# Storing 21 groups of the turned adjacency as fp32 words in place of fp16 pairs

## What is computed

```python
# one: hyperbolic mean
XW = mobius_matvec(W, X); gamma = 2.0 / (1.0 - sum(XW * XW))
two_mean = (A_hat @ (gamma * XW)) / (A_hat @ (gamma - 1.0))
# two: symmetric normalisation
support = norm_adj @ x;  out = support @ W.T + b
# three: diffusion and attention masked by adj
diffusion = adj_norm @ x - x
attn = softmax(beta * (x @ x.T / norms) * adj, axis=1)
out = diffusion + sigmoid(alpha) * (attn @ x - x)
# four: messages into a GRU cell
agg = adj @ states;  msg = relu(agg @ W_msg.T + b_msg);  out = gru(msg, states)
```

## Time and profile before

| | us |
|---|---|
| median of 3 runs | 1311.12 (1306.46 to 1311.75) |
| the profiled execution | 1309.65 |
| its span, first to last instruction | 1307.9 |
| PE busy | 1227.0 (94%) |
| DVE busy | 770.7 (59%) |
| ACT busy | 685.3 (52%) |
| POOL busy | 460.1 (35%) |

### The profile page before, as it was taken

The page is one execution under the profiler, slowest core; times in us unless marked ns, Lnnn a source line. Parts: engine busy times, 40 slices in busy tenths (PEclk is TensorE's granted clock), DMA queues, the critical chain, the costliest instruction groups (busy, mean ns, idle before and its releaser), DMA issues.

```text
span 1307.9 us, 20934 instructions
## 1 busy us (share of the span) xinstructions
PE 1227.0 (94%) x7980; PEld 789.5 (60%) x7980; DVE 770.7 (59%) x1769; ACT 685.3 (52%) x995; POOL 460.1 (35%) x433
## 2 busy tenths in 40 slices
PE   5889999999999989869999999999999889999996
PEld 4888888887884544425555656555655544444442
DVE  6856665655643352687787878787878860122213
ACT  6555555555442222168778787878787530123222
POOL 4012231222123232325566665657565560000000
PEclk9899999999999999979999999999999999999998
DMA  9999999999978979466777777877776849978870
GB/s 304 358 416 415 406 397 377 386 350 357 352 288 320 387 299 353 177 241 247 269 265 274 258 268 267 285 268 287 269 278 213 302 178 365 390 272 315 312 267 24
DMA packets 113524, 394.20 MB, mean 301 GB/s; under 512 B 9872, under 2 KB 23440, under 8 KB 91536
## 3 DMA queue, kind: packets, MB, share of 16 engines
q1 hardware_dynamic: 105232, 388.80, 79.7%
q10 hardware_dynamic: 8192, 4.06, 1.1%
HBM read 319.95 MB, written 72.88 MB: 300 GB/s over the span
## 4 chain that ended last, share of the span: by engine, by line
PE 78%; DVE 8%; ACT 5%; DMA 4%; issue 4%; POOL 2%; POOLq 0%; SPq 0%; ACTq 0%; DVEq 0%
PE strip_b L688 8%; PE acc L629 6%; PE acc L630 6%; PE acc L636 6%; PE acc L707 4%; PE acc L705 4%; PE acc L704 4%; PE acc L703 4%; PE acc L605 4%; PE mid L605 4%; PE strip_b L580 3%; PE strip_a L580 3%; PE acc L603 2%; PE mid L603 2%; PE strip_a L671 2%
## 5 line engine op out<-in xcount | busy, mean ns | idle before, releaser
L1224 POOL TENSOR_TENSOR parts<-arena,parts 128x512 f16<-128x512 f32 x237 | 275.6, 1172 | 196.3 <-ACT parts L980 192.4
L980 ACT ACTIVATE parts<-arena 128x512 f16<-128x512 f32 x256 | 158.5, 624 | 111.1 <-DVE arena L1635 102.6
L1635 DVE SCALAR_TENSOR_TENSOR arena<-parts,dis,strip_b 128x512 f32<-128x512 f16 x256 | 188.9, 743 | 29.7 <-PE strip_b L688 22.5
L629 PE MATMUL acc<-arena,Y 128*128 128x512 f16 x428 | 162.8, 380 | 3.5 <-DMA arena<-adj_t 2.0
L688 PEld LDWEIGHTS strip_b<-ident,arena 128*128 128x128 f32 x1024 | 128.2, 142 | 60.9 <-DVE arena L1626 5.4
L688 PE MATMUL strip_b<-ident,arena 128*128 128x128 f32 x1024 | 155.4, 275 | 8.8 <-ACT arena L975 5.7
L630 PE MATMUL acc<-arena,Y 128*128 128x512 f16 x428 | 162.6, 380 | 0.0
L636 PE MATMUL acc<-arena,Y 128*128 128x512 f16 x428 | 162.5, 380 | 0.0
L969 ACT ACTIVATE arena<-arena,neg_peak 128x2048 f32<-128x2048 f32 x64 | 127.3, 1989 | 5.2 <-DVE neg_peak L1605 5.2
L1201 POOL TENSOR_TENSOR sc<-sc,power 128x4 f32<-128x4 f32 x31 | 31.5, 1016 | 279.6 <-DVE sc L1454 279.6
L975 ACT ACTIVATE arena<-arena,weight 128x2048 f32<-128x2048 f32 x57 | 113.4, 1989 | 2.6 <-DVE weight L1619 2.6
(11 more groups left out here) (332 smaller groups left out, 2559.1 us busy)
## 6 DMA issues: line engine op xcount, KB each, us to landing
arena<-adj_t SPq DMA_DIRECT2D x107, 1024.0 KB, 6.0
arena<-in_adj SPq DMA_DIRECT2D x64, 1024.0 KB, 9.5
arena<-in_adj SPq DMA_DIRECT2D x128, 512.0 KB, 5.8
parts<-adj_t SPq DMA_DIRECT2D x128, 512.0 KB, 7.3
adj_t<-parts SPq DMA_DIRECT2D x37, 1024.0 KB, 8.2
adj_t<-arena SPq DMA_DIRECT2D x27, 1024.0 KB, 9.2
scratch<-v ACTq DMA_DIRECT2D x8, 256.0 KB, 10.6
arena<-scratch SPq DMA_DIRECT2D x8, 256.0 KB, 4.6
```

The source lines that it names most:

```text
L629: pe.matmul(to, y_high, high, start=j == 2 * FIRST[l][s], stop=False)
L980: act.activation(part_h[:, b % 4, :], mixed[b % G_SLOTS], ACT.Copy).then_inc(high_done, 1)
L1224: pool.tensor_tensor(part_l[:, b % 4, :], mixed[b % G_SLOTS], part_h[:, b % 4, :], ALU.subtract).then_inc(low_done, 1)
L1635: dve.scalar_tensor_tensor(mixed[b % G_SLOTS], kept_slot(n % KEPT_SLOTS)[:, b % 2, 0, :], dis[:, j:j + 1], strip_b[:, b % 2, :], ALU.mult, ...
```

## The change

The 21 groups that layer two does not read back (`whole(s, g)`: g <= s - 2) are kept in DRAM as fp32 words, as many bytes as the two fp16 parts.

- Layer one: for these 42 pairs ACT first copies the scaled strip as fp32 into a ring slot of its own (`whole0`), then makes the high part from that slot into a second, "working" slot; DVE makes the low part from the two slots. PE's turn of pair n+2 waits for that copy and not for the low part. The whole slot is stored, the working slot is not; ring places are given in the order of the list `HOLDS`.
- Layer three: for the 84 whole blocks `mix` reads the fp32 block, and the product with the kept low part (L703) is left out.
- Layer four: for the 42 whole pairs ACT (`split3_high`) and DVE (`split3_low`) make high and low part in one of the six `kept_slot` places, one turn ahead in their programs; PE waits for that, and SP's next load into the slot waits for the split.

```diff
+def whole(s, g):
+    return g <= s - 2
+HOLDS = []
+for _s in range(SLABS):
+    for _g in range(GROUPS):
+        HOLDS += [("working" if whole(_s, _g) else "pair", _s * GROUPS + _g)] \
+            + ([("whole", _s * GROUPS + _g)] if whole(_s, _g) else [])
+WHOLE3 = [n for n in range(TURNS3) if whole(TURNS[3][n][0], TURNS[3][n][1] // 2)]
...
+                elif l == 3 and 2 * (n - TURNED_SLOTS) in WHOLE3:
+                    sp.wait_ge(low3_done, WHOLE3.index(2 * (n - TURNED_SLOTS)) + 2)
...
-                    sp.wait_ge(low_done, 2 * n + 2)
-                    sp.dma_start(adj_t[s, c], ring_slot(n)).then_inc(stored[n % RING_SLOTS], 16)
+                    if whole(s, c):
+                        sp.wait_ge(whole_done, wholes_done(2 * n + 1))
+                        sp.dma_start(adj_t[s, c], ring_slot(n, "whole")).then_inc(stored[store_hold(n) % RING_SLOTS], 16)
+                    else:
+                        sp.wait_ge(low_done, 2 * n + 2)
+                        sp.dma_start(adj_t[s, c], ring_slot(n)).then_inc(stored[store_hold(n) % RING_SLOTS], 16)
...
-                if n >= 2:
+                if n >= 2 and is_whole((n - 2) // PAIRS, (n - 2) % PAIRS):
+                    pe.wait_ge(whole_done, wholes_done(n - 2))
+                elif n >= 2:
                     pe.wait_ge(low_done, n - 1)
...
+                if l == 3 and n in WHOLE3:
+                    pe.wait_ge(low3_done, WHOLE3.index(n) + 1)
+                    pair = kept_slot(WHOLE3.index(n) % KEPT_SLOTS)
...
-                pe.matmul(to, Y[:, j, YD:YD + D], kept_slot(b // 2 % KEPT_SLOTS)[:, b % 2, 1, :], start=j == 0, stop=False)
-                pe.matmul(to, Y[:, j, 0:D], part_h[:, b % 4, :], start=False, stop=False)
+                apart = not is_whole(s, j // 2)
+                if apart:
+                    pe.matmul(to, Y[:, j, YD:YD + D], kept_slot(b // 2 % KEPT_SLOTS)[:, b % 2, 1, :], start=j == 0, stop=False)
+                pe.matmul(to, Y[:, j, 0:D], part_h[:, b % 4, :], start=j == 0 and not apart, stop=False)
...
+            def whole0(n):
+                g = n // 2
+                act.wait_ge(turned_up, n + 1)
+                hold_free(hold_of(g, "whole"))
+                act.activation(whole_pair(ring_slot(g, "whole"), n), strip[n % 2][:], ACT.Copy,
+                               scale=A_SCALE).then_inc(whole_done, 1)
+
+            def split3_high(n):
+                at = WHOLE3.index(n)
+                act.wait_ge(group_in[n // 2 % TURNED_SLOTS], groups_loaded(3, n // 2))
+                act.wait_ge(product, product_base[3] + (WHOLE3[at - KEPT_SLOTS] + 1 if at >= KEPT_SLOTS else 0))
+                act.activation(kept_slot(at % KEPT_SLOTS)[:, :, 0, :],
+                               whole_pair(turned_in[:, n // 2 % TURNED_SLOTS, :], n), ACT.Copy).then_inc(high3_done, 1)
...
+                if is_whole(n // PAIRS, n % PAIRS):
+                    act.wait_ge(whole_done, wholes_done(n))
+                    act.activation(ring_pair(n)[:, :, 0, :], whole_pair(ring_slot(g, "whole"), n),
+                                   ACT.Copy).then_inc(high_done, 1)
...
+                if is_whole(s, m):
+                    whole0(n)
                 high0(n)
...
+                if n + 1 in WHOLE3:
+                    split3_high(n + 1)
                 for k, s in hooks(3, n - ACT_LEAD):
...
+                if is_whole(n // PAIRS, n % PAIRS):
+                    dve.tensor_tensor(pair[:, :, 1, :], whole_pair(ring_slot(n // 2, "whole"), n), pair[:, :, 0, :],
+                                      ALU.subtract).then_inc(low_done, 1)
...
+            def split3_low(n):
+                at = WHOLE3.index(n)
+                held = kept_slot(at % KEPT_SLOTS)
+                dve.wait_ge(high3_done, at + 1)
+                dve.tensor_tensor(held[:, :, 1, :], whole_pair(turned_in[:, n // 2 % TURNED_SLOTS, :], n), held[:, :, 0, :],
+                                  ALU.subtract).then_inc(low3_done, 1)
...
+                kept = kept_whole(n % KEPT_SLOTS)[:, b % 2, :] if is_whole(b // NB, j // 2) \
+                    else kept_slot(n % KEPT_SLOTS)[:, b % 2, 0, :]
-                dve.scalar_tensor_tensor(mixed[b % G_SLOTS], kept_slot(n % KEPT_SLOTS)[:, b % 2, 0, :], dis[:, j:j + 1],
+                dve.scalar_tensor_tensor(mixed[b % G_SLOTS], kept, dis[:, j:j + 1],
                                          strip_b[:, b % 2, :], ALU.mult, ALU.add).then_inc(mixed_done, 1)
...
+                if n + 1 in WHOLE3:
+                    split3_low(n + 1)
                 for k, s in hooks(3, n - DVE_LEAD):
```

More of the change, by code:

```diff
@@ L189, in spare, with hold_of, ring_slot, whole_pair @@
             return arena[:, FULL + SLAB * n:FULL + SLAB * (n + 1)]
-        def ring_slot(g):
-            at = g % RING_SLOTS
+        def hold_of(g, kind):
+            return [at for at, (what, one) in enumerate(HOLDS) if one == g and (what == "whole") == (kind == "whole")][0]
+        def ring_slot(g, kind="pair"):
+            at = hold_of(g, kind) % RING_SLOTS
             return ring_head[:, at, :] if at < 4 else ring_tail[:, at - 4, :]
+        def whole_pair(held, n):
+            return held[:, 2 * UNIT * (n % 2):2 * UNIT * (n % 2 + 1)].bitcast(F32).rearrange("p (b w) -> p b w", w=SLAB)
         def split_pair(held, n):
@@ L336, in split_done, with stores_until, last_stores, store_hold @@
             return PAIRS * SLABS + b + 1
-        def held_stored(g):
-            return stored[g % RING_SLOTS], 16 * (g // RING_SLOTS + 1)
+        def stores_until(hold):
+            return 16 * sum(HOLDS[at][0] != "working" for at in range(hold % RING_SLOTS, hold + 1, RING_SLOTS))
+        def last_stores(slot):
+            return 16 * sum(HOLDS[at][0] != "working" for at in range(slot, len(HOLDS), RING_SLOTS))
+        def store_hold(g):
+            return hold_of(g, "whole" if whole(g // GROUPS, g % GROUPS) else "pair")
+        def held_stored(g):
+            hold = store_hold(g)
+            return stored[hold % RING_SLOTS], stores_until(hold)
+        def wholes_done(n):
+            return sum(whole(i // PAIRS, i % PAIRS // 2) for i in range(n + 1))
+        def is_whole(s, m):
+            return whole(s, m // 2)
         def unit_of(k):
@@ L883, in y_high, with hold_free @@
                                scale=scale).then_inc(y_hi, 1)
+            def hold_free(hold):
+                if hold >= RING_SLOTS:
+                    what, one = HOLDS[hold - RING_SLOTS]
+                    if what != "working":
+                        act.wait_ge(stored[hold % RING_SLOTS], stores_until(hold - RING_SLOTS))
+                    if what == "whole":
+                        act.wait_ge(low_done, 2 * one + 2)
+                    else:
+                        act.wait_ge(product, 2 * one + 2)
+            def whole0(n):
[10 more added lines that the diff above has]
+                               whole_pair(turned_in[:, n // 2 % TURNED_SLOTS, :], n), ACT.Copy).then_inc(high3_done, 1)
             def high0(n):
```

22 lines of the change are left out of this document (14 added, 8 removed).

## The result

The changed kernel takes 1315.21 us (median of 12 runs) against 1309.13 us before: ratio 1.0045, 95% interval 1.0036 to 1.0055. The forecast was 1306 us; the true change is small, but it has the other sign. The profiled execution took 1316.75 us, span 1314.9, 7.0 us more than the span before. One execution of the experiments (of E12's ten) took 7343 us; the intervals leave it out, and without it E12's median is 1312.7.

A forecast was written before the change was run, and what follows sets the result against it. The prediction took PE to bound the kernel. Its terms, -10.9 - 1.5 + 6.3 + 1.5 = -4.6 us on the profiled 1309.65, gave 1305.0; with the runs' median 1.5 higher it forecast 1306 us, range 1297 to 1316.

The forecast's parts named there:

- second rival: Layer three: steps stay at 1.91 us because ACT and DVE cannot follow; +5.1 us, 1316 us, chance 0.15.
- the step that failed: Layer one, six slab entries: a second ACT copy makes PE stand 1.05 us longer each, +6.3 us (bounds +4, +11).
- signs of being wrong: PE waits on ACT or DVE inside layer one's or at most layer four's whole units, or layer-three steps near 1.95 us.
- Layer three, slabs 2 to 6: 60 whole blocks each drop a 0.216 us product, less 2.0 us lost in layer norm: -10.9 us (bounds -12.9, -2).
- Slab 7: Layer three's last slab: 24 dropped products, 5.2 us for PE, mostly limited by others: -1.5 us (bounds 0, -5.0).
- Both resources named: Layer three, slab 7: DVE (31.1 us busy) and DMA (31 us) leave at most 5.0 of 36.1 us.
- Layer four: The splits of 42 pairs are hidden except at turn 32, the first whole turn: +1.5 us (bounds 0, +3).
- The port: Layer one's slab changes: DVE's low part meets a POOL instruction, 0.78 us longer, 4.7 us in all; 1311 us, chance 0.07.
- ACT late in layer one: Doubled copies reach PE in every whole pair, up to 1.05 us each, 38 us more; 1344 us, chance 0.08.
- Layer three does not follow: Layer three: steps of 1.91 us, as ACT and DVE are at 90%; +5.1 us, 1316 us, chance 0.15.

The follow-up runs named there:

- E12: Kernel before, with half of an additional ScalarE copy (512 of 1,024 elements a partition) at each of six layer-one slab entries: 1312.9 us.
- E3: Kernel before, with ScalarE making the high part of pair 1 of slabs 2 to 7 in layer one twice: 1317.6 us.
- E7: Changed kernel, with layer three's left-out product replaced by one of the same size with other operands: 1324.0 us.
- E4: Changed kernel, with group 0 of each slab left as fp16 parts, so 15 fp32 groups in place of 21: 1306.2 us.
- E10: Changed kernel, with layer four's first six group loads issued behind layer three's last pair, not between its pairs: 1316.6 us.
- E1: Changed kernel, with the last slab's accumulators read one pair earlier in layer one: 1310.9 us.
- E11: Changed kernel, with layer four's splits put behind the row steps of the same turn, not ahead of them: 1315.2 us.
- E8: Changed kernel, without layer four's splits and the waits for them, fp32 words multiplied as they are: 1311.5 us.
- E5: Changed kernel, with whole groups from group 1 on and none in slab 7, so 10 groups in place of 21: 1304.6 us.
- E2: Kernel before, with the last slab's accumulators read one pair earlier in layer one, no fp32 group: 1306.8 us.
- E6: Changed kernel, with whole groups from group 1 on (15) and accumulators read one pair earlier in slabs 3 to 7: 1303.9 us.

## Why the prediction was wrong, point by point

Between the -4.6 us of the sum and the +7.0 of the profiles stand 11.6 us: 7.2 in layer one, 1.5 in layer three's slabs 2 to 6, 1.9 in slab 7 and 0.9 in layer four. The 1306 started from a median of three runs, 1311.12; twelve gave 1309.13, so the forecast looks about 2 us nearer than it was. That 1315.2 lies within 1297 to 1316 is luck: the top of that range came from the second rival, whose steps of 1.91 us did not occur.

**Layer one: the step that failed** is "6 x 1.05 = +6.3 us ... it does not come back", with +11 as its upper bound. Measured: +13.5. What was worked out of the earlier trace rows held: the place, the six entries, the order of the instructions and the length of the wait (2.45 against "about 2.3") were right, and 6 x 1.18 = 7.1 us are that term. The other 6.5 us are the clock: four falls of 1.6. The term took PE's idle time at a price of its own length and put what comes behind it at nothing; E3 and E12 show that behind waits of 2.32 us time is lost as well, at two entries of five, and behind waits of up to 1.93 us it isn't. Neither bound held such a thing, since the earlier trace rows showed clock 1.00 throughout layer one. With these 6.5 us the forecast of 1306 becomes 1312.5. None of the prediction's signs of being wrong appeared, since all of them were waits and steps, and none was the granted clock.

**Layer three, slabs 2 to 6: right, a little too high.** -9.4 against -10.9. Steps of 1.73 us and the price of a matmul are exact (E7). The layer norm took 60 x 0.216 - 9.4 = 3.5 us, not 2.0: 0.25 of them in slab 4, where none were expected, 1.1 in slab 5, as worked out, and 2.15 in slab 6. E4 loses the same 3.5 with 40 blocks.

**Slab 7: nothing, as one bound had it.** +0.4 against -1.5. Both resources named are behind it: with the loads out of the way 2.2 of the 5.2 us reach the end of the slab (E10), and the rest goes in PE's waits on GpSimd and VectorE.

**Layer four: right, as far as the splits go.** +2.0 and +0.4 later against +1.5. The splits' part is 1.1 us at turn 32 (1.3 to 1.6 in E1, E7 and E11), where the term had put it, and 0.3 at turn 85; both go in E8. The 0.85 ahead of turn 32 comes before any split and is 0.26 at most in E1, E7 and E11; what makes it stays open. At turn 32 the load landed at 1119.25, and PE was due at 1120.88 by its wait of 0.96: a lead of 1.6 us (1 was worked out) against a split of 2.3. What was costed at nothing, the row work queued behind the split, is what PE's record names there, 0.2 us after the split's own data.

**The rivals.** The port: no low part at an entry was lengthened (VectorE's instruction of slab 6 takes 1.23 us). The rule cited (the Trainium skill, SBUF — State Buffer, Who interferes with whom) does show once, in slab 7 at 394.07, where a low part took 1.84 us in place of 1.22 while GpSimd's L1283 ran until 394.83; PE lost nothing by it. ACT late in layer one: not seen by PE between the entries, but E1 shows it hidden behind them, 1.4 us a slab. "Layer three does not follow" named 1316, near the result, for a reason that the steps of 1.73 us refute.

## What to carry to other kernels

Count what an added instruction delays at the places where the pipeline drains, not where it is full: 30 doubled copies cost 0.1 us and the 12 of group 0 cost 13.5, and choosing which groups are treated (E4, E5) turned a loss of 0.45% into a gain of 0.34%. When PE's wait grows, ask whether its clock will still be whole behind it, since a fall (1.6 us) can cost more than the wait grew by (1.18). A stage in which loads and other engines stand close behind PE keeps only what they leave, in slab 7 nothing of 5.2 us: there the cheaper form is to leave it alone.

## What the runs showed of the hardware

PE's granted clock fell to 0.50 (1.2 of 2.4 GHz) for 3.41 us right behind waits of 2.05 to 2.45 us at the entries into slabs, in a stretch in which PE was otherwise full, and never there behind waits of 0.9 to 1.93 us; a fall cost about 1.6 us. The length of the one wait does not settle it: behind 2.32 us the clock fell at two entries of five, and a wait of 1.98 us early in slab 1 had no fall behind it in twelve profiles and one in E1 and in E2, where a wait of 1.25 us stands just ahead of it. At turn 12 of layer four the clock fell behind waits for a load of 2.4 us (E6), 3.2 (E4) and 5.9 (E10), and not behind the 1.2 to 1.7 us of the other profiles. Profiles with the same waits don't all fall at the same entries. A small delay ahead of PE can therefore cost its own length (1.18 us) or more than twice that (2.8), and only the granted clock in the profile tells which.
